# Macaron block on one core: turned exponentials by VectorE instead of TensorE and ScalarE, keys and values by separate products, the latent stored interleaved

## The chip, the core and the metric

The kernel runs on one core of one Trainium2 chip. The metric is the device time of one execution in microseconds (us); lower is better. In the rows, PE is TensorE (PEld its weight loads), DVE is VectorE, ACT is ScalarE, POOL is GpSimd and SP is SyncE, whose queue issues the loads and stores.

## What is computed

Input x has 8 batches of 512 tokens of 256 features. The block is a feed-forward part at half weight, an attention part, and the same feed-forward part again with the same weights:

```
x = x + 0.5 * ffn(layernorm(x))
x = x + attn(layernorm(x))        # softmax over the 8 groups of a query and a key token
x = x + 0.5 * ffn(layernorm(x))

ffn(x):   # H = 16 heads, HD = 16, L = 64, E = 8 experts
    h   = rmsnorm(x) * gamma1
    q   = (h @ Wq + bq).reshape(b, t, 16, 16)
    kv  = ((h @ Wdown + bdown) @ Wup + bup).reshape(b, t, 16, 32)
    k, v = split(kv)
    att = softmax(einsum('bthd,btgd->bthg', q, k) / sqrt(16))     # within ONE token: head h against head g
    out = einsum('bthg,btgd->bthd', att, v).reshape(b, t, 256)
    x   = x + out @ Wo + bo
    h2  = rmsnorm(x) * gamma2
    return x + sum over e of softmax(h2 @ Wg + bg)[e] * (h2 @ We[e])
```

All of it is in float32. The large products of the feed-forward part are made of a rounded high part and a rest (`_hi`, `_lo`), so that each takes three matmuls of TensorE's rounded float32 type.

The part that is changed is the small attention inside `ffn`: each token has its own 16 x 16 scores. The latent is `h @ Wdown + bdown`, 64 numbers for each token.

## The kernel before

**Jobs and pairs.** A feed-forward pass over one batch (512 tokens, NT = 4 tiles of 128) is a job. Jobs 0 to 7 are the first feed-forward part, 8 to 15 the second; the attention over all batches lies between. A job's per-token attention works in two pairs of tiles (`p` = 0, 1), so there are 32 pairs, `c = 2 * job + p`.

**Order.** Every piece of work is a step with an engine, a cost in ns and the steps that it waits for (`all_steps`). `all_orders` plays them through and gives each engine a fixed order: whenever an engine is free, it takes the ready step of the highest rank. The tables `SOONER` (an addition to the rank by name) and `FIRST` (by job) shift the ranks. PSUM banks 5, 6 and 7 go round among the steps in `RING`; banks 3 and 4 together go to those in `WIDE`; banks 0 to 2 go round among the experts. On the chip, each engine works through its list strictly in that order and waits at semaphores.

**One pair, before.** Its steps are, with the lines of the profile:

1. `down` (PE), `la_hi` (ACT L1258), `la_lo` (DVE L1041, L1043) and `la_one` (POOL L1572) make the latent `la` for the whole job, 64 rows high part and 64 rows rest, column = token.
2. `kv` (PE, `psum<-wu,la` and `psum<-wu,la_one`): for each tile two matmuls of 512 columns, keys and values of one tile together, into banks 3 and 4.
3. `kv_turn` (DVE L1064, L1066): two stream transposes, one for keys and one for values, into one of three buffers `kvc`. A stream transpose turns each 32 x 32 block in place.
4. `expand` (ACT L1260 and POOL L1512, four operations each by the string `EXPAND`): the turned keys and values times a mask, into `kvx`.
5. `scores` (PE L662): 32 small products. `top` (DVE L1076, L1080): subtracts the maximum. `exp` (ACT L1264).
6. `turn_probs` (PE L789): four 128 x 128 transposes of the exponentials into a bank of the ring. `at` (ACT L1275): four copies from there into `at`, the weights of the next product.
7. `attend` (PE L673): 32 small products into banks 3 and 4, with the sum of the exponentials as a 17th column. `mult` (DVE L1089, L1091): reciprocal of the sum, and the product with it into `on`. `out_turn` (DVE L1100): a stream transpose into `ot`.
8. `oT` (PE L803), `wo` (PE `psum<-wo,oT`), `x1`, `half` (DVE L1116) and so on, up to the experts: 16 steps `expert` for each job (PE L491 `psum<-we,h`, six matmuls of 512 columns each), which DVE (`add`, L1165) and ACT (`y`, L1339) empty in turn.

`turn_nothing` (PE L702) is a number of transposes whose result nobody reads.

## Time and profile before

| | before |
|---|---|
| median of 3 runs | 1039.59 us (1038.6 to 1041.17) |
| the profiled execution's own time | 1039.06 us |
| its span (first to last instruction) | 1037.2 us |
| PE busy | 986.5 us, 95% |
| DVE busy | 823.4 us, 79% |
| POOL busy | 768.3 us, 74% |
| ACT busy | 675.7 us, 65% |

Busy time is the union of an engine's instructions; consecutive matmuls overlap, so the duration of one (272 ns for a 128-column transpose) is longer than the distance from its start to the next one's start. What a group of matmuls takes of TensorE is read as the distance between starts in the timeline. The profile is of one execution, so what follows is reckoned against its 1039.06 us, 1.86 us more than its span.

### The profile page before, as it was taken

The numbers are of one execution on the slowest core, as the hardware profiler recorded it, in microseconds if no ns is written. First come the engines' busy times: TensorE is split into PE (matmuls) and PEld (weight loads), VectorE is DVE, ScalarE is ACT, GpSimd is POOL, SyncE is SP. The second block draws the span as 40 slices with busy tenths as digits, with TensorE's granted clock in tenths as the row PEclk, the third lists the DMA queues.
The fourth block names the chain that finished last, engine by engine and source line by source line (L and its number), as shares of the span: only waits on it lengthen the run. The fifth ranks groups of instructions, "written<-read, shape, count | busy, mean of one in ns | idle before, by whom it ended". The sixth has DMA issues, their size and how long they took to land.

```text
span 1037.2 us, 28141 instructions
## 1 busy us (share of the span) xinstructions
PE 986.5 (95%) x11200; PEld 769.0 (74%) x11200; DVE 823.4 (79%) x1239; ACT 675.7 (65%) x1411; POOL 768.3 (74%) x789
## 2 busy tenths in 40 slices
PE   7699999999999989999999999888999999999998
PEld 6578778888788766667667667556788788888786
DVE  7588788788877459999999999997877877776754
ACT  4586575675776357778778777686775665755752
POOL 7777787786774549899899898997676775865734
PEclk8799999999999999999999999999999999999999
DMA  6210000000000000000000000000000000000001
GB/s 195 84 43 1 2 2 1 3 2 1 2 2 2 1 1 2 2 2 1 2 1 3 2 2 2 2 1 2 3 1 23 22 2 22 22 2 22 22 2 41
DMA packets 7966, 14.20 MB, mean 14 GB/s; under 512 B 1945, under 2 KB 5660, under 8 KB 7838
## 3 DMA queue, kind: packets, MB, share of 16 engines
q1 hardware_dynamic: 7838, 12.41, 3.6%
q8 instruction: 91, 1.49, 0.6%
q14 instruction: 37, 0.30, 0.1%
HBM read 8.21 MB, written 4.19 MB: 12 GB/s over the span
## 4 chain that ended last, share of the span: by engine, by line
PE 70%; DVE 10%; POOL 5%; issue 5%; ACT 3%; DVEq 0%; ACTq 0%; POOLq 0%
PE psum L491 48%; PE psum L892 5%; PE psum L902 4%; PE psum L918 4%; DVE oT L1191 3%; DVE late L1197 3%; PE psum L662 2%; PE psum L673 2%; POOL kvx L1585 1%; PE psum L803 1%; PE psum L818 1%; POOL late L1585 1%; PE psum L789 1%; DVE hT L1183 1%; POOL rs L1478 1%
## 5 line engine op out<-in xcount | busy, mean ns | idle before, releaser
L491 PE MATMUL psum<-we,h 128*128 128x512 f32 x1536 | 393.6, 400 | 1.8 <-DVE X L1165 1.2
L491 PEld LDWEIGHTS psum<-we,h 128*128 128x128 f32 x1536 | 278.1, 188 | 63.7 <-issue 2.9
L1401 ACT ACTIVATE kvx<-psum 128x1024 f32<-128x1024 f32 x126 | 129.1, 1025 | 62.2 <-PE psum L902 60.5
L1339 ACT ACTIVATE late<-psum,gate 128x256 f32<-128x256 f32 x252 | 104.9, 468 | 97.4 <-PE psum L491 51.6
L1165 DVE SCALAR_TENSOR_TENSOR X<-psum,gate,X 128x256 f32<-128x256 f32 x260 | 124.4, 479 | 54.0 <-PE psum L491 42.3
L1191 DVE TENSOR_REDUCE oT<-psum 128x128 fp32r<-128x1024 f32 x128 | 154.7, 1219 | 14.7 <-PE psum L892 14.4
L1543 POOL TENSOR_TENSOR late<-late 128x512 f32<-128x512 f32 x63 | 81.4, 1293 | 111.1 <-ACT late L1339 111.1
L1197 DVE TENSOR_REDUCE late<-kvx 128x256 f32<-128x2048 f32 x63 | 143.4, 2276 | 0.3 <-POOL late L1585 0.2
L1585 POOL TENSOR_TENSOR kvx<-kvx,late 128x2048 f32<-128x2048 f32 x32 | 125.3, 3916 | 16.4 <-ACT late L1408 16.3
L1585 POOL TENSOR_TENSOR late<-kvx,late 128x2048 f32<-128x2048 f32 x31 | 121.8, 3928 | 19.7 <-ACT late L1408 19.7
L1260 ACT ACTIVATE kvx<-kvcs,mask 128x512 f32<-128x512 f32 x132 | 86.4, 730 | 37.7 <-DVE kvcs L1066 35.2
L902 PE MATMUL psum<-oT,neg_id 128*128 128x512 f32 x256 | 88.6, 427 | 13.6 <-DVE oT L1191 13.3
L1512 POOL TENSOR_SCALAR kvx<-kvcs,mask 128x512 f32<-128x512 f32 x124 | 85.9, 713 | 8.4 <-DVE kvcs L1066 8.3
L902 PEld LDWEIGHTS psum<-oT,neg_id 128*128 128x128 f32 x256 | 40.6, 188 | 28.5 <-DVE oT L1191 19.2
L1275 ACT ACTIVATE at<-psum 64x256 f32<-64x256 f32 x128 | 48.5, 379 | 17.3 <-PE psum L789 15.8
L892 PEld LDWEIGHTS psum<-late 32*128 32x128 f32 x1024 | 36.7, 185 | 27.0 <-issue 27.0
L892 PEld LDWEIGHTS psum<-kvcs 32*128 32x128 f32 x1024 | 36.7, 185 | 26.5 <-issue 23.9
L491 PEld LDWEIGHTS psum<-wq,hT 128*128 128x128 f32 x384 | 51.8, 198 | 5.4 <-issue 2.6
L491 PE MATMUL psum<-wq,hT 128*128 128x256 f32 x384 | 53.5, 290 | 2.1 <-DVE hT L1035 2.0
L1290 ACT ACTIVATE late<-late 128x256 f32<-128x256 f32 x64 | 26.2, 411 | 44.2 <-DVE late L1111 44.2
L1548 POOL TENSOR_TENSOR X<-X,late 128x256 f32<-128x256 f32 x63 | 46.6, 740 | 9.0
L892 PE MATMUL psum<-kvcs 32*128 32x128 f32 x1024 | 49.3, 295 | 3.1 <-ACT kvx L1401 2.4
(169 smaller groups left out, 1950.9 us busy)
## 6 DMA issues: line engine op xcount, KB each, us to landing
X<-in_L_attn_hidden_states SPq DMA_DIRECT2D x8, 512.0 KB, 5.5
out<-X SPq DMA_DIRECT2D x7, 512.0 KB, 2.6
X<-in_L_ffn_We SPq DMA_DIRECT2D x2, 1024.0 KB, 10.7
out<-X SPq DMA_DIRECT2D x1, 384.0 KB, 2.3
kvx<-in_L_ffn_Wq SPq DMA_DIRECT2D x1, 256.0 KB, 3.4
kvx<-in_L_ffn_Wup SPq DMA_DIRECT2D x2, 128.0 KB, 3.0
kvx<-in_L_ffn_Wo SPq DMA_DIRECT2D x8, 32.0 KB, 2.6
X<-in_L_attn_Wk SPq DMA_DIRECT2D x1, 256.0 KB, 2.6
```

Source lines behind the costliest of these rows:

```text
L491: ins = e.matmul(out_ap, l, r, start=(n == 0), stop=(n == len(terms) - 1))
L892: ins = e.matmul(psum[:, pair(half) + bank, n * HQN:(n + 1) * HQN], qk[b % 2][rows, 1, hg, m * P:(m + 1) * P], qk[b % 2][rows, 0, hg, q0:q ...
L902: ins = e.matmul(psum[:, bank, :].rearrange("p (g n) -> p g n", n=HQN), neg_id[:, :], mr[g // 2 % 2][:, queries(g)].unsqueeze(1).to_broadc ...
L1165: e.scalar_tensor_tensor(out=xi, in0=psum[:, u % 3, w * D:(w + 1) * D], scalar=gate[k % 2][:, i, 2 * n + w:2 * n + w + 1], in1=xi, op0=ALU ...
L1191: e.tensor_reduce(mr[g // 2 % 2][:, queries(g)], heads(g), AX.X, ALU.max).then_inc(a_max, 1)
L1197: e.tensor_reduce(rec[u % 2][:, :], exponentials(u)[:, :, :], AX.X, ALU.add).then_inc(a_total, 1)
L1260: expand(e, k, "A", lambda o, src, m_: e.activation(o, src, ACT.Copy, scale=m_))
L1339: e.activation(y[:, n // 2 * 2 + w, :], psum[:, u % 3, w * D:(w + 1) * D], ACT.Copy, scale=gate[k % 2][:, i, 2 * n + w:2 * n + w + 1]).the ...
L1401: e.activation(exponentials(u)[:, queries(g), :], heads(g), ACT.Exp, scale=float(D) ** -0.5).then_inc(a_exp, 1)
L1512: expand(e, k, "P", lambda o, src, m_: e.tensor_scalar(o, src, m_, 1.0, ALU.mult, ALU.mult))
L1543: own.step(e.tensor_tensor(y[:, 0:2, :], y[:, 0:2, :], y[:, 2:4, :], ALU.add))
L1585: e.tensor_tensor(prob[u % 2][:, :, :].rearrange("p g n -> p n g"), exponentials(u)[:, :, :], rec[u % 2][:, :].unsqueeze(2).to_broadcast([ ...
```

## The change

- `turn_probs` is gone. `at` is now on DVE: two stream transposes, each of 64 partitions x 512, from the exponentials in SBUF straight into `at`. For this the order of tokens in the small products, the permutation `perm` and the rows of `Wo` (reordered before the launch, so that one load replaces eight) are other ones.
- `kv` becomes `key` for each pair (four matmuls of 256 columns, a bank of the ring) and `val` for each job (eight matmuls of 256 columns, banks 3 and 4). `kv_turn` becomes `key_turn` for each pair (one transpose) and `val_turn` for each job (two). `expand` becomes `key_P`, `key_A`, `val_P`, `val_A` (two operations each, of the same 128 x 512). The keys' half of `kvx` is free again after the `scores` two pairs before, no longer after the `attend`.
- The latent is written interleaved: the four tiles' columns lie side by side (`by_tile`), so that `la_hi` and `la_lo` write, and `key` reads its weights, at every fourth word. `val` reads its weights in one piece.
- `mult` and `out_turn` change places: `out_turn` turns the raw 544 columns out of PSUM into `raw_ot` (SBUF), which frees banks 3 and 4, and `mult` then takes reciprocal and product from SBUF to SBUF.
- One of the four groups of `turn_nothing` at the start (13 transposes ahead of the second `attend`) is gone. `SOONER` and `FIRST` are new tables.

```diff
-EXPAND = "PPAAAPPA"
+EXPAND = {"key": "PPAA", "val": "APPA"}
...
-            put("PE", 945, ("kv", s, p), ("la_lo", s, part(p)), ("la_one", s, part(p)), ...)
-            put("DVE", 2005, ("kv_turn", s, p), ("kv", s, p), ...)
+            put("PE", 470, ("key", s, p), ("la_lo", s, part(p)), ("la_one", s, part(p)), ...)
+            put("DVE", 1030, ("key_turn", s, p), ("key", s, p))
...
-            put("PE", 435, ("turn_probs", c), ("exp", c), ("attend", c - 1))
-            put("ACT", 1450, ("at", c), ("turn_probs", c))
-            put("PE", 1085, ("attend", c), ("at", c), ("mult", c - 1))
-            put("DVE", 1000, ("mult", c), ("attend", c), ("out_turn", c - 1))
-            put("DVE", 700, ("out_turn", c), ("mult", c), ("oT", s - 1, p))
+            put("DVE", 1450, ("at", c), ("exp", c), ("attend", c - 1))
+            if not p:
+                put("PE", 940, ("val", s), ("la_lo", s, part(1)), ("la_one", s, part(1)), ...)
+                put("DVE", 2005, ("val_turn", s), ("val", s), ...)
+            put("PE", 1085, ("attend", c), ("at", c), *((f"val_{w}", c) for w in "PA"), ("out_turn", c - 1))
+            put("DVE", 750, ("out_turn", c), ("attend", c))
+            put("DVE", 900, ("mult", c), ("out_turn", c), ("oT", s - 1, p))
...
-                elif piece == ("attend", 1):
-                    turn_nothing(e, 13)
...
+                elif name == "val":
+                    e.wait_ge(s_la_one, done(k))
+                    e.wait_ge(s_la_lo, done(k))
+                    for i in range(NT):
+                        cols = slice(i * P, (i + 1) * P)
+                        terms = [(la[:, cols], wu[:, 0, D:]), (la_one[:, cols], wu[0:HALF + 2, 1, D:])]
+                        ins = product(e, psum[:, 3 + i // 2, (i % 2) * D:(i % 2 + 1) * D], terms)
+                    ins.then_inc(s_val, 1)
...
+        def by_tile(t):
+            return t[:, :].rearrange("p (n i) -> p i n", i=NT)
...
-                    own.step(e.tensor_tensor(la[up, cols], psum[low, b, cols], la[low, cols].bitcast(F32), ALU.subtract))
-                    e.wait_ge(own.sem, own.n)
-                    e.tensor_tensor(la[up, cols], psum[up, b, cols], la[up, cols].bitcast(F32), ALU.add).then_inc(s_la_lo, 1)
+                    own.step(e.tensor_tensor(kept[up], made[low], kept[low].bitcast(F32), ALU.subtract))
+                    e.wait_ge(own.sem, own.n)
+                    e.tensor_tensor(kept[up], made[up], kept[up].bitcast(F32), ALU.add).then_inc(s_la_lo, 1)
...
+                elif name == "at":
+                    c = piece[1]
+                    if c:
+                        e.wait_ge(s_attend, c)
+                    else:
+                        e.wait_ge(s_pad, 4)
+                    e.wait_ge(s_exp, c + 1)
+                    for z in range(2):
+                        half = slice(z * HALF, (z + 1) * HALF)
+                        ins = e.transpose(at[half, :, z, :].rearrange("p (u n) h -> p n u h", u=2),
+                                          ex[c % 2][half, :].rearrange("p (n g) -> p n g", g=NR))
+                    ins.then_inc(s_at, 1)
...
+                    src = psum[:, 3:5, 0:NR // 2 * (HD + 1)].rearrange("p a (t d) -> p d a t", d=HD + 1)
+                    e.transpose(raw_ot, src).then_inc(s_raw, 1)
+                elif name == "mult":
...
+                    own.step(e.reciprocal(r_, raw_ot[:, HD]))
+                    e.wait_ge(own.sem, own.n)
+                    e.tensor_tensor(ot[c % 2][:, :, :].rearrange("p z (d h) -> p d z h", h=H), raw_ot[:, 0:HD],
+                                    r_.unsqueeze(1).to_broadcast([P, HD, 2, H]), ALU.mult).then_inc(s_ot, 1)
```

**TensorE's order in the middle of the first feed-forward part, before.** The names are those of the tiles: `kvx,qc` is `scores`, `kvx,at` is `attend`, `ident,late` is `turn_probs` where four stand alone, `we,h` the experts, `ident,ct` a transpose of the gate, `ident,xs` of the next job's input.

```order
L662 MATMUL psum<-kvx0,qc0 32x64 x32
L831 MATMUL psum<-ident,ct 128x16 x4
L491 MATMUL psum<-we,h21 128x512 x6
L491 MATMUL psum<-we,h20 128x512 x6
L789 MATMUL psum<-ident,late 128x128 x4
L491 MATMUL psum<-we,h20 128x512 x6
L662 MATMUL psum<-kvx1,qc1 32x64 x32
L673 MATMUL psum<-kvx0,at 32x68 x32
L491 MATMUL psum<-we,h20 128x512 x6
L789 MATMUL psum<-ident,late 128x128 x4
L749 MATMUL psum<-ident,xs 128x128 x8
```

The same place of a job in the changed kernel:

```order
L677 MATMUL psum<-kvx0,qc0 32x64 x32
L505 MATMUL psum<-we,h20 128x512 x24
L677 MATMUL psum<-kvx1,qc1 32x64 x32
L687 MATMUL psum<-kvx0,at 32x68 x32
L505 MATMUL psum<-we,h20 128x512 x12
L761 MATMUL psum<-ident,xs 128x128 x4
L818 MATMUL psum<-perm,late 128x8x16 x4
L761 MATMUL psum<-ident,xs 128x128 x4
L505 MATMUL psum<-we,h20 128x512 x6
L687 MATMUL psum<-kvx1,at 32x68 x32
```

The two rows of four transposes per job are gone; from the first `scores` to the first `attend` stand four expert steps instead of three, and there are again three places in a job where small products begin behind large ones.

**VectorE's order at the same place, before.** `mx` is `top`, `rc` and the row behind it `mult`, `late<-late` `out_turn`, `X<-psum,gate` `add`, which empties an expert's bank.

```order
L1076 TENSOR_REDUCE mx1<-psum 128x32
L1080 TENSOR_TENSOR late<-psum,mx1 128x512
L1089 RECIPROCAL rc<-psum 128x32
L1091 TENSOR_TENSOR late<-psum,rc 128x512
L1100 STREAM_TRANSPOSE late<-late 128x16x2x16
L1165 SCALAR_TENSOR_TENSOR X<-psum,gate1,X 128x256 x2
```

And in the changed kernel, where `at<-late` is the new `at` and `late<-psum 128x544` the new `out_turn`:

```order
L1126 STREAM_TRANSPOSE at<-late 64x16x2x16 x2
L1210 SCALAR_TENSOR_TENSOR X<-psum,gate0,X 128x256 x4
L1111 TENSOR_REDUCE mx1<-psum 128x32
L1115 TENSOR_TENSOR late<-psum,mx1 128x512
L1135 STREAM_TRANSPOSE late<-psum 128x544
L1142 RECIPROCAL rc<-late 128x32
L1144 TENSOR_TENSOR late<-late,rc 128x16x2x16
L1126 STREAM_TRANSPOSE at<-late 64x16x2x16 x2
L1210 SCALAR_TENSOR_TENSOR X<-psum,gate0,X 128x256 x2
```

Each pair has one more row of VectorE (two instructions of `at`) ahead of the `add` that empties an expert's bank, and the rows of `mult` stand behind the transpose instead of ahead of it.

## Rows read from the trace of the kernel before

**Rows 1.** The page: busy time of each engine, and the chain that ended last.

```profile
PE 986.5 (95%) x11200; PEld 769.0 (74%) x11200; DVE 823.4 (79%) x1239; ACT 675.7 (65%) x1411; POOL 768.3 (74%) x789
...
PE 70%; DVE 10%; POOL 5%; issue 5%; ACT 3%; DVEq 0%; ACTq 0%; POOLq 0%
```

**Rows 2.** The chain in order of time: start, length (us), what; one piece of each job.

```profile
201.16 13.55 PE psum L491 x76
...
241.70 13.55 PE psum L491 x76
...
828.26 13.55 PE psum L491 x76
...
869.03 13.56 PE psum L491 x76
```

**Rows 3.** Busy us of PE, PEld, DVE, ACT, POOL in those two stretches; PEclk.

```profile
201.16:241.70 40.54, 40.51 (x453) 33.41 (x453) 32.86 (x67) 25.67 (x62) 30.29 (x44) 1.00 0.01 2
828.26:869.03 40.77, 40.54 (x454) 33.42 (x453) 31.18 (x59) 25.67 (x63) 28.70 (x40) 1.00 0.04 15
```

**Rows 4.** Timeline of PE around the two turn_probs of a job: start, length.

```profile
228.20 0.60 PE L789 MATMUL psum<-ident,late 128*128 128x128 f32 x4
228.55 1.63 PE L491 MATMUL psum<-we,h 128*128 128x512 f32 x6
...
233.64 0.63 PE L789 MATMUL psum<-ident,late 128*128 128x128 f32 x4
234.11 1.04 PE L749 MATMUL psum<-ident,xs 128*128 128x128 f32 x8
```

**Rows 5.** Timeline of PE: matmuls of 512 and of 256 columns.

```profile
205.20 1.56 PE L491 MATMUL psum<-we,h 128*128 128x512 f32 x6
206.60 1.56 PE L491 MATMUL psum<-wo,oT 128*128 128x256 f32 x12
207.99 1.09 PE L491 MATMUL psum<-hT,wd 128*128 128x512 f32 x4
```

**Rows 6.** Timeline of PE: first matmul of a kv, and what follows its four.

```profile
220.57 0.40 PE L491 MATMUL psum<-wu,la 128*128 128x512 f32 x1
...
221.52 0.85 PE L491 MATMUL psum<-h,wg 128*16 128x512 f32 x3
```

**Rows 7.** DVE, 201.16 to 241.70, by line: busy us, mean ns, idle before.

```profile
L1064 DVE STREAM_TRANSPOSE kvcs<-psum 128x512 f32<-128x512 f32 x2 | 2.3, 1136 | 0.0
...
L1100 DVE STREAM_TRANSPOSE late<-late 128x512 f32<-128x512 f32 x2 | 2.2, 1086 | 0.2
...
L1091 DVE TENSOR_TENSOR late<-psum,rc 128x512 f32<-128x512 f32 x2 | 1.4, 692 | 0.1
...
L1041 DVE TENSOR_TENSOR la<-psum,la 64x512 fp32r<-64x512 f32 x1 | 0.7, 685 | 0.0
```

**Rows 8.** Timeline: half (DVE) and rms2 (POOL) in two jobs.

```profile
92.27 1.19 DVE L1116 SCALAR_TENSOR_TENSOR X<-late,X 128x1024 f32<-128x1024 f32 x1
...
92.87 0.65 POOL L1536 TENSOR_SCALAR rms<-ssq 128x4 f32<-128x4 f32 x1 [0.64 <-ACT late L1290]
...
208.99 1.23 DVE L1116 SCALAR_TENSOR_TENSOR X<-late,X 128x1024 f32<-128x1024 f32 x1
...
210.12 0.20 POOL L1536 TENSOR_SCALAR rms<-ssq 128x4 f32<-128x4 f32 x1 [2.13 <-ACT late L1290]
```

**Rows 9.** Timeline of job 0 (ACT, PE) and job 8 (ACT); in brackets idle before.

```profile
29.86 0.61 ACT L1264 ACTIVATE late<-late 128x512 f32<-128x512 f32 x1
31.80 1.55 ACT L1275 ACTIVATE at<-psum 64x256 f32<-64x256 f32 x4 [1.33 <-PE psum L789]
...
51.48 1.58 PE L702 MATMUL psum<-ident 128*128 128x128 f32 x13
53.00 1.15 PE L673 MATMUL psum<-kvx,at 128*32 128x68 f32 x64
...
704.54 0.77 ACT L1275 ACTIVATE at<-psum 64x256 f32<-64x256 f32 x2 [0.87 <-PE psum L789]
```

**Rows 10.** The page: the maximum over groups in the attention (1024 PSUM words by partition).

```profile
L1191 DVE TENSOR_REDUCE oT<-psum 128x128 fp32r<-128x1024 f32 x128 | 154.7, 1219 | 14.7 <-PE psum L892 14.4
```

283 lines of the change are left out of this document (147 added, 136 removed).

## Prediction

> **What bounds the kernel now.** I read the page first: TensorE is busy 95% of the span, VectorE 79%, GpSimd 74%, and the chain that ended last runs 70% through TensorE [rows 1]. Then the chain in order of time. In both feed-forward parts it repeats the same long piece of expert matmuls once for each job: at 201.16 and 241.70, so 40.54 us a job, and at 828.26 and 869.03, so 40.77 us [rows 2]. Then the busy time in just those two stretches: TensorE 40.51 of 40.54 and 40.54 of 40.77 at a granted clock of 1.00, VectorE 32.86 and 31.18, ScalarE 25.67 in both, GpSimd 30.29 and 28.70 [rows 3]. The reader is to see that in a settled job nothing but TensorE's own work sets the time. What is taken from TensorE there shortens the kernel one for one, as long as no other engine comes up to its 40 us. VectorE is the nearest, 7.7 us below. In jobs 0 and 8 it is different: there the experts of an earlier job are missing as filling, and TensorE waits for the steps of the pair.
>
> **What the change takes from TensorE.** A job has two `turn_probs`. By the distance between starts the first takes 228.55 - 228.20 = 0.35 us and the second 234.11 - 233.64 = 0.47 us, since the next group's weights come later there [rows 4]. Together 0.82 us. I count 14 settled jobs (1 to 7 and 9 to 15): 14 x 0.82 = 11.5 us. Job length then would be 39.7 and 39.95 us.
>
> The split products cost nothing by rows. Six matmuls of 512 columns take 206.60 - 205.20 = 1.40 us, twelve of 256 columns 207.99 - 206.60 = 1.39 us, with new weights for each [rows 5]: the price is by column. A `kv` takes 221.52 - 220.57 = 0.95 us [rows 6], 1.90 for a job; four plus four plus eight matmuls of 256 columns take 16 x 0.116 = 1.86. No row shows a weight load that reads every fourth word. At worst each of the 8 in a job costs one more product's time, 0.93 us a job, which would eat the whole gain; at best nothing. I take nothing, because the loads run ahead under the product before them, as in rows 5.
>
> Small products begin behind large ones at three places in a job both before and after, so changing between them costs the same.
>
> **What it puts on VectorE**, for a job. Two transposes of `at` for each pair, four in a job. No row has a transpose that both reads and writes in order. The upper bound is the transpose from SBUF to SBUF, 1.09 us, the lower the plain operation of 512 words, 0.69 [rows 7]: 2.8 to 4.4 us. `out_turn` now handles 544 words out of PSUM: between 0.73 (0.692 x 544 / 512) and 1.21 (1.136 x 544 / 512) against 1.09 [rows 7], so -0.7 to +0.2 for two. For a plain read, hopping through PSUM costs nothing: 1024 words take 1.219 us in the maximum over groups [rows 10], 1.23 in `half`, which reads SBUF in order [rows 8]. Key and value turns are four transposes as before: nothing. `mult` keeps its two instructions: nothing by itself. `la_lo` writes at every fourth word: 0.685 each [rows 7] at best; at worst the ratio 1.09 / 0.69 more, +0.8 for two. The sum is +2.1 to +5.4 us. VectorE then has 35.0 to 38.3 us of work in a job of 39.7. I take 1.09 for `at`, the nearest row (it too writes in runs of 16 words), and the middle for the rest: +4.5, so 37.4. That is 94%: below TensorE, but with little room.
>
> [...]
>
> **A new collision.** The product in `mult` used to read PSUM and a small SBUF tensor; now both inputs lie in SBUF. The one operation of that kind in a job is `half`. When GpSimd had a 0.20 us operation start under it, that operation took 0.65 us and ended at 93.52, just behind `half` at 93.46; in a later job it started at the end of `half` and took 0.20 [rows 8]. So they exclude each other. In the feed-forward part GpSimd is busy 75% of the time with 44 instructions of 0.69 us on average [rows 3]; a `mult` waits for half of one with that chance, 0.26 us, and GpSimd waits as long for it. That is 0.5 us a job for VectorE, 37.9 in all. The Trainium skill (SBUF — State Buffer, section SBUF: two separate sides) names this as a lock that VectorE and GpSimd hold for a whole instruction; rows 8 agree.
>
> Queued behind `at` and `mult` on VectorE are the `add`s that empty an expert's bank. While VectorE waits (`at` for the exponentials on ScalarE, `mult` for GpSimd), TensorE runs on two more expert steps, 2.8 us, and then stops. Half of VectorE's spare time is used up, so some of this will reach TensorE. I take about one such collision a job, 0.3 us, 14 x 0.3 = +4.2 us; the bounds are 0 and the 0.82 of rival 2.
>
> **What is gone from ScalarE** (two times 1.55 us a job [rows 9]) is hidden, as it has 15 us to spare [rows 3]. Expansion is in eight equal operations as before, split four and four: nothing.
>
> **Jobs 0 and 8.** There the way over TensorE is waited for: ScalarE stood idle 1.33 us before `at` in job 0 and 0.87 in job 8 [rows 9]. Both go: -2.2 us. The transposes in place of the 1.55 us of copies [rows 9] take 1.4 to 2.2 us: nothing. The 13 filling transposes took 53.00 - 51.48 = 1.52 us [rows 9]; part of that may have filled a wait that stays, so I count -1.0. Keys get to `scores` one transpose earlier, but the values now wait for the whole latent; I set these off against each other, with 2 us either way.
>
> **Sum:** 1039.06 - 11.5 - 2.2 - 1.0 + 4.2 = 1028.6 us. The profiled execution is 0.5 us below the median of 1039.59, which changes nothing here.
>
> **The rivals.**
> 1. *All of it comes through and more.* VectorE's additions vanish in its spare time (-4.2), the starts gain 2 us more, and ScalarE's relief frees expert banks sooner: about 1021. For it speaks that TensorE waits for nobody in the settled jobs now.
> 2. *The gain is given back.* TensorE's 0.82 a job turns into waiting: for the latent, whose two VectorE writes may be 0.8 us longer in a chain that ends at `key`, or for slower weight loads, or for expert banks behind `at`. The job stays at 40.5 us, only the starts gain: 1039.06 - 3.2 = 1036.
> 3. *VectorE becomes the bound, the kernel gets slower.* Today it is idle 7.7 us in a job. If half of that, 3.9, is waiting which its order cannot avoid (for a product that has just been made, for ScalarE's half of a step), a job takes 37.4 + 3.9 = 41.3 us instead of 40.54: 14 x 0.8 = +11, less the 3.2 of the starts: 1047. It decides from the point at which VectorE's work and those waits together exceed 40.5 us; at 1.09 us for each new transpose that is 3.2 us of waits. Against it: a VectorE that waits for a full TensorE loses nothing by having more to do meanwhile.
> 4. *The transposes leave TensorE but their time was hidden anyway.* Excluded by rows 3: TensorE has 0.03 us idle in the job.
>
> **How the numbers follow.** Forecast (1023 to 1033) 0.45, rival 1 0.15, rival 2 0.22, rival 3 0.18. A measurement of this kernel tells a change from none at about 0.3%, 3.1 us. Faster: 0.45 + 0.15 + half of rival 2 = 0.71. The same: the other half, 0.11. Slower: 0.18. The range goes from 1018, rival 1 with the starts' 2 us and a little more, to 1045, most of the way to rival 3: some 0.05 lies below and 0.13 above.
>
> **What the profile afterwards would show.** Right: the expert piece of the chain repeats every 39.7 to 40.1 us in the middle of both parts, TensorE idle under 0.4 us there, VectorE at 36 to 38.5 us. `at` at 0.7 to 1.1 us each; `out_turn` under 1.2. `mult`'s product sometimes well over 0.69, or GpSimd operations stretched under it. The first `at` of job 0 done before 33.35 us, where it ended so far. Rival 2: job length 40.5, with TensorE waiting before `psum<-wu,la` for `la_lo`, or its 256-column matmuls with `la` further apart than 0.12. Rival 3: TensorE idle before the experts because of VectorE's `add`, VectorE above 39 us. What would make me wrong altogether is a new order that starves TensorE in places which the settled jobs of before say nothing of, above all jobs 0 and 8.

## The result, and the profile after

The changed kernel takes 1044.96 us (median of four runs, 1044.74 to 1045.93) against 1039.3 us before on the same chip: a ratio of 1.0053, 95% interval 1.0041 to 1.0066. A later comparison gave 1.0057 (1.0041 to 1.0074). It is slower, by 5.5 to 6 us, where 11 us less were forecast. The profiled execution took 1045.93 us, with a span of 1044.1. One execution of all those below, 3174.89 us in run e3, fell in a slow state and is left out of its ratio, though not of its median of five.

The page: busy time of each engine, and the chain that ended last.

```profile
PE 994.7 (95%) x11187; PEld 781.9 (75%) x11187; DVE 876.1 (84%) x1303; ACT 642.4 (62%) x1283; POOL 772.8 (74%) x789
...
PE 71%; DVE 17%; issue 6%; POOL 3%; ACT 2%; DVEq 0%; ACTq 0%; POOLq 0%
```

Against [rows 1] TensorE has 13 instructions less in sum and is busy 8.2 us longer. Something that it still does has become dearer, and by more than the 11.5 us that `turn_probs` took. VectorE is busy 53 us more, and its part of the chain went from 10% to 17%.

The chain in order of time (start, length, what), with one piece of each job:

```profile
162.68 10.79 PE psum L505 x58
...
245.69 10.79 PE psum L505 x58
...
879.06 10.00 PE psum L505 x60
920.32 10.00 PE psum L505 x60
```

Between the first two lie two jobs, so a job takes 83.01 / 2 = 41.5 us, and 41.26 in the second feed-forward part; before it was 40.54 and 40.77 [rows 2]. The busy time in these two stretches (PE, PEld, DVE, ACT, POOL, then PEclk):

```profile
162.68:245.69 83.01, 82.36 (x905) 67.87 (x905) 71.00 (x141) 47.17 (x109) 61.50 (x88) 1.00 0.01 2
879.06:920.32 41.26, 41.01 (x453) 33.95 (x454) 34.52 (x63) 23.82 (x55) 28.65 (x40) 1.00 0.04 15
```

TensorE is still full (82.36 of 83.01) and VectorE has 35.5 us a job, not 37.4. So the settled job is not bound by VectorE, as rival 3 had it, and the reader has to look inside TensorE's own work. Its timeline at one pair's `key` (four products) and the `val` behind it (eight):

```profile
181.03 0.51 PE L505 MATMUL psum<-wu,la 128*128 128x256 f32 x1
181.38 0.40 PE L505 MATMUL psum<-wu,la_one 66*128 66x256 f32 x1
181.61 0.40 PE L505 MATMUL psum<-wu,la 128*128 128x256 f32 x1
...
182.07 0.28 PE L505 MATMUL psum<-wu,la 128*128 128x256 f32 x1
...
182.31 0.29 PE L505 MATMUL psum<-wu,la 128*128 128x256 f32 x1
```

From the third product of `key` to the first of `val`, 182.07 - 181.61 = 0.46 us for two products, 0.23 each. Within `val`, 182.31 - 182.07 = 0.24 for two, 0.12 each, the pitch of [rows 5]. The same products, the same columns, the granted clock at 1.00 in both; they differ in the weights, which `key` takes at every fourth word of the latent and `val` from adjacent ones. The first product takes 0.12 us more (181.38 - 181.03 = 0.35). A job has two `key`, so it pays 8 x 0.115 = 0.92 us, which is the very bound of the prediction that I set aside.

VectorE in 162.68 to 245.69 (two jobs), by line and form; busy us, mean ns:

```profile
L1126 DVE STREAM_TRANSPOSE at<-late 64x512 f32<-64x512 f32 x8 | 5.6, 695 | 0.1
...
L1144 DVE TENSOR_TENSOR late<-late,rc 128x512 f32<-128x512 f32 x4 | 3.2, 789 | 0.1
L1135 DVE STREAM_TRANSPOSE late<-psum 128x544 f32<-128x544 f32 x4 | 3.0, 742 | 0.0
...
L1067 DVE TENSOR_TENSOR la<-psum,la 64x512 fp32r<-64x512 f32 x2 | 2.2, 1088 | 2.0 <-ACT la L1303 2.0
L1069 DVE TENSOR_TENSOR la<-psum,la 64x512 fp32r<-64x512 f32 x2 | 2.2, 1083 | 0.1
```

The new transposes are at the lower end of my bounds (0.70 us), and `la_lo` is at the upper (1.09 instead of 0.69). ScalarE's `la_hi`, which I had not priced, went from 0.58 to 1.10 us too (from 120 to 340 us):

```profile
L1303 ACT ACTIVATE la<-psum 64x512 fp32r<-64x512 f32 x5 | 5.5, 1095 | 1.1 <-PE psum L505 1.1
```

Two places outside the settled jobs stand out. In job 0 (start, length; DVE, then POOL, then PE):

```profile
32.43 5.42 DVE L1144 TENSOR_TENSOR late<-late,rc 128x512 f32<-128x512 f32 x1
...
30.56 2.76 POOL L1547 TENSOR_SCALAR kvx<-kvcs,mask 128x512 f32<-128x512 f32 x4
33.28 0.43 POOL L981 TENSOR_SCALAR kvx<-mask 128x128 f32<-128x128 f32 x1
33.58 3.71 POOL L1528 TENSOR_TENSOR we<-X,we 128x512 fp32r<-128x512 f32 x3
...
37.99 0.63 PE L818 MATMUL psum<-perm,late 128*128 128x128 f32 x4 [3.50 <-DVE late L1144]
```

The product in `mult` lasts 5.42 us, where the others take a median of 0.70. It begins during the third of eight GpSimd instructions that stand one against the other (four `kvx`, one mask, three `we`), and ends at 37.85, just behind the last of them, which ends at 37.29. TensorE waits 3.50 us for it.

And at the passage from the attention to job 8, where TensorE comes to `attend` 16 late:

```profile
709.85 2.04 PE L687 MATMUL psum<-kvx,at 128*32 128x68 f32 x64 [2.79 <-issue]
...
728.06 0.48 PE L505 MATMUL psum<-wu,la 128*128 128x256 f32 x1 [1.71 <-DVE la L1069]
```

The busy time of the stretch behind it (PE, PEld, DVE, ACT, POOL, then PEclk):

```profile
710.00:715.00 5.00, 5.00 (x135) 4.83 (x131) 2.74 (x5) 1.51 (x4) 4.41 (x9) 0.50 0.01 3
```

Before `attend` 16 TensorE is idle for 2.79 us; from 710 to 715 the granted clock then stands at 0.50, its lower level of 1.2 GHz. Before the change the stretches from 700 to 720 us all show 1.00. On VectorE, job 9's statistics and a turn of keys now stand ahead of `top` 16. At 728.06 TensorE waits 1.71 us for `la_lo`.

### The profile page after: what moved, and what is told of

The parts are those of the page before. It is cut to its first block, busy times and chain, and to the rows that moved or that the text cites. A ratio compares the mean times of both kernels' runs of the same rounds, so it can differ in the third digit from the quotient of the medians.

```text
span 1044.1 us, 28145 instructions
## 1 busy us (share of the span) xinstructions
PE 994.7 (95%) x11187; PEld 781.9 (75%) x11187; DVE 876.1 (84%) x1303; ACT 642.4 (62%) x1283; POOL 772.8 (74%) x789
## 4 chain that ended last, share of the span: by engine, by line
PE 71%; DVE 17%; issue 6%; POOL 3%; ACT 2%; DVEq 0%; ACTq 0%; POOLq 0%
PE psum L505 49%; PE psum L907 5%; PE psum L917 4%; PE psum L933 4%; DVE oT L1236 3%; DVE late L1242 3%; PE psum L687 2%; PE psum L677 2%; DVE at L1126 2%; DVE X L1210 2%; PE psum L818 1%; PE psum L833 1%; POOL late L1624 1%; DVE kvcs L1100 1%; DVE late L1135 1%
## 5 line engine op out<-in xcount | busy, mean ns | idle before, releaser
L1624 POOL TENSOR_TENSOR kvx<-kvx,late 128x2048 f32<-128x2048 f32 x32 | 125.5, 3923 | 16.5 <-ACT late L1443 16.4
L917 PEld LDWEIGHTS psum<-oT,neg_id 128*128 128x128 f32 x256 | 40.5, 188 | 29.6 <-DVE oT L1236 20.3
L505 PE MATMUL psum<-wo,oT 128*128 128x256 f32 x384 | 51.6, 284 | 1.9 <-DVE oT L1150 1.9
L505 PEld LDWEIGHTS psum<-wo,oT 128*128 128x128 f32 x384 | 48.7, 189 | 4.9 <-issue 2.5
```

What stands on the lines that cost most here:

```text
L505: ins = e.matmul(out_ap, l, r, start=(n == 0), stop=(n == len(terms) - 1))
L917: ins = e.matmul(psum[:, bank, :].rearrange("p (g n) -> p g n", n=HQN), neg_id[:, :], mr[g // 2 % 2][:, queries(g)].unsqueeze(1).to_broadc ...
L1624: e.tensor_tensor(prob[u % 2][:, :, :].rearrange("p g n -> p n g"), exponentials(u)[:, :, :], rec[u % 2][:, :].unsqueeze(2).to_broadcast([ ...
```

## The experiments

The expectations name theories by letters. W: TensorE's weight loads set the time. V: VectorE does. C: the granted clock costs it at jobs 0 and 8. O: the order of VectorE's steps at job 8 does. X: the product of pair 0 waits for GpSimd.

Each ratio is to runs of the kernel before on the same chip. Where two versions are set against each other, it is by these ratios, and the changed kernel stands at 1.0055, the middle of its two comparisons.

| run | what | us | ratio, 95% |
|---|---|---|---|
| e12 | changed kernel once more | 1044.17 | 1.0057 (1.0041 to 1.0074) |
| e1 | key reads adjacent words | 1034.68 | 0.9959 (0.9944 to 0.9974) |
| e2 | latent stored plainly | 1029.13 | 0.9911 (0.9897 to 0.9926) |
| e3 | product first, out of PSUM | 1043.59 | 1.0043 (1.0028 to 1.0059) |
| e4 | filling ahead of attend 1 and 16 | 1042.35 | 1.0044 (1.0027 to 1.0060) |
| e5 | four transposes back at each pair | 1053.87 | 1.0159 (1.0137 to 1.0180) |
| e6 | kernel before, kv at every fourth word | 1040.40 | 1.0023 (1.0013 to 1.0032) |
| e7 | top 16 ahead of the statistics | 1044.60 | 1.0064 (1.0049 to 1.0079) |
| e8 | two latents | 1033.06 | 0.9953 (0.9938 to 0.9967) |
| e9 | e8 with filling at three places | 1029.03 | 0.9910 (0.9893 to 0.9926) |
| e10 | e9 with the rules of e7 and e3 | 1035.84 | 0.9966 (0.9953 to 0.9979) |
| e15 | latent written in stored order | 1037.87 | 0.9997 (0.9987 to 1.0006) |
| e16 | e9 with the rule of e7 | 1032.99 | 0.9952 (0.9935 to 0.9969) |
| e17 | e9 written in stored order | 1030.80 | 0.9914 (0.9898 to 0.9931) |
| e18 | e15 with the filling | 1036.53 | 0.9977 (0.9967 to 0.9986) |
| e20 | product first in pair 0 alone | 1039.47 | 1.0014 (1.0001 to 1.0027) |
| e19 | e9 with that | 1027.90 | 0.9894 (0.9874 to 0.9914) |

**The changed kernel again: e12.**

> The changed kernel itself once more, beside the two below and on the same chip, so that they can be set against it without going over the kernel before. 1042 to 1046 us, ratio 1.004 to 1.007.

It came out as before. In its profile the first expert of job 8 begins at 730.10 us, in the first one at 732.45, so two profiles of one kernel differ by 2 us at this place.

**The weight loads: e1.**

```diff
-                        terms = [(by_tile(la)[:, i], wu[:, 0, 0:D]), (by_tile(la_one)[:, i], wu[0:HALF + 2, 1, 0:D])]
+                        whole = parts_of(k, B) == 1
+                        own_cols = slice(i * P, (i + 1) * P)
+                        first, one = (la[:, own_cols], la_one[:, own_cols]) if whole else (by_tile(la)[:, i], by_tile(la_one)[:, i])
+                        terms = [(first, wu[:, 0, 0:D]), (one, wu[0:HALF + 2, 1, 0:D])]
```

> The changed kernel, except that in the 14 whole jobs (1 to 7 and 9 to 15) the key product takes its weights from the latent in one adjacent piece of 128 words instead of every fourth word. The latent is still stored interleaved, so the keys of these jobs belong to the wrong tokens; all else is as it was. Theory W (the weight load at every fourth word is what takes the gain back): key's eight 256-column matmuls of a job go from 0.235 to 0.12 us, 0.92 us a job, and the wait of 0.1 to 0.3 us ahead of the first goes too: 14 x 1.0 to 1.2 = 14 to 17 us, so 1028 to 1031 us and a job of 40.4 us. Rival V (VectorE with its new transposes, longer latent writes and the exclusion with GpSimd sets the job's length, the slow loads lie in time that would be waited anyway): 1042 to 1046 us, with TensorE idle more before the experts and attend.

From 1.0055 to 0.9959: 10 us faster, where I expected 14 to 17. Timeline of PE at the same `key`:

```profile
179.01 0.39 PE L505 MATMUL psum<-wu,la 128*128 128x256 f32 x1
179.24 0.28 PE L505 MATMUL psum<-wu,la_one 66*128 66x256 f32 x1
179.36 0.28 PE L505 MATMUL psum<-wu,la 128*128 128x256 f32 x1
```

The pitch is 0.12 us again. Two jobs of the first part and one of the second:

```profile
161.16:242.33 81.17, 80.65 (x906) 66.15 (x905) 70.55 (x141) 46.72 (x109) 61.81 (x88) 1.00 0.01 2
866.83:907.21 40.38, 40.20 (x453) 33.12 (x454) 34.21 (x63) 23.68 (x55) 28.86 (x40) 1.00 0.04 15
```

A job takes 40.58 and 40.38 us, 0.92 and 0.88 less than in the changed kernel. Fourteen times that is more than 10 us; the profiled execution took 1030.90 us, 3.8 less than the median. The loads are the largest loss. But with them repaired a job of the first part is still as long as before the change (40.54), though its two `turn_probs` are gone: here TensorE is idle for 0.26 us a job instead of 0.03, and busy only 0.2 us less. This is a second loss, of which more below.

**The latent's layout as a whole: e2.**

```diff
         def by_tile(t):
-            return t[:, :].rearrange("p (n i) -> p i n", i=NT)
+            return t[:, :].rearrange("p (i n) -> p i n", i=NT)
```

> The changed kernel with the latent stored in the plain order: la_hi, la_one and la_lo write, and key and val read, one adjacent piece for each tile, in all 16 jobs. Queries, keys and values then pair the wrong tokens; the amount of work is the same. Theory W: the gain is that of the plain key load (1028 to 1031 us), with up to 2 us more at jobs 0 and 8, whose latent is on the way that is waited for: 1026 to 1031. Rival V: VectorE is relieved by 2 x 0.4 us a job of la_lo, and GpSimd and ScalarE by 0.3 and 0.5 us, so if VectorE's load sets the job's length this gives at least 14 x 0.4 = 5 us more than the key load alone, 1023 to 1026 if both matter, about 1038 if only VectorE does.

15 us faster than the changed kernel, and 5 faster than e1. The key loads alone are not all that the interleaving costs.

**The load by itself: e11.** Behind TensorE's last instruction:

```diff
+            for hop in (1, 2, 4):
+                for wide in (128, 256, 512):
+                    for n in range(24):
+                        o = n % hop
+                        w_ = la[:, :].rearrange('p (n i) -> p i n', i=hop)[:, o, n % (4 // hop) * P:n % (4 // hop) * P + P]
+                        e.matmul(psum[:, 3, 0:wide], w_, wu[:, 0, 0:wide], start=True, stop=True, skip_group_check=True)
```

> The changed kernel with nine runs of 24 products each put behind TensorE's last instruction, with the latent as weights and nothing to wait for, written to a bank that nobody reads: weights taken in adjacent words, at every second and at every fourth word, each with products of 128, 256 and 512 columns. Only their pitch counts, not the kernel's time. Theory W: adjacent, the pitch is by columns, 0.06, 0.12 and 0.23 us; at every fourth word the load lasts 0.235 us whatever follows, so 0.235 for 128 and for 256 columns, and 0.235 to 0.25 for 512, where it is covered; every second word in between or like adjacent. Rival (a fixed time added to each load): at every fourth word 0.12 us above the adjacent pitch at each width, 0.18, 0.235 and 0.35.

One row for each run of 24 products, from its first start to that of the next (busy PE and PEld, with those that overlap an edge counted on both sides; then PEclk): adjacent, every second and every fourth word, each with 128, 256 and 512 columns.

```profile
1039.74:1042.36 2.62, 2.62 (x24) 2.62 (x24) 1.00 0.31 115
1042.36:1045.27 2.91, 2.91 (x27) 2.91 (x26) 1.00 0.00 0
1045.27:1050.88 5.61, 5.61 (x26) 4.54 (x25) 1.00 0.00 0
1050.88:1053.70 2.82, 2.82 (x26) 2.81 (x24) 1.00 0.03 6
1053.70:1056.66 2.96, 2.96 (x27) 2.96 (x27) 1.00 0.00 0
1056.66:1062.26 5.60, 5.60 (x27) 4.75 (x25) 1.00 0.00 0
1062.26:1067.69 5.43, 5.43 (x25) 5.43 (x25) 0.87 0.00 0
1067.69:1073.35 5.66, 5.66 (x25) 5.66 (x26) 0.53 0.00 0
1073.35:1078.88 5.53, 5.53 (x24) 5.53 (x24) 1.00 0.00 0
```

The last row ends with the start of its 24th product, so that 23 pitches lie in it; the others are divided by 24: adjacent words 0.109, 0.121 and 0.234 us; every second word 0.118, 0.123 and 0.233; every fourth word 0.226, 0.236 and 5.53 / 23 = 0.240. So every second word costs next to nothing, and at every fourth a load lasts 0.23 us whatever its product's columns. It is a duration of the load, hidden under a product that is as long, and not a fixed addition; the rival's 0.18 and 0.35 are not there. With 128 columns even adjacent words give 0.109, where I expected 0.06 by columns: the pitch does not follow the columns down to there. In the two rows ahead of the last the granted clock falls to its lower level while nothing but such loads and short products ran, and the pitch stays at 0.23: the load does not go with that clock.

**The same load under a longer product: e6**, an edit of the kernel before.

```diff
-                        terms = [(la[:, i * P:(i + 1) * P], wu[:, 0, :]),
-                                 (la_one[:, i * P:(i + 1) * P], wu[0:HALF + 2, 1, :])]
+                        mixed = lambda t: t[:, :].rearrange("p (n i) -> p i n", i=NT)[:, i]
+                        plain = lambda t: t[:, i * P:(i + 1) * P]
+                        of_tile = mixed if parts_of(k, B) == 1 else plain
+                        terms = [(of_tile(la), wu[:, 0, :]), (of_tile(la_one), wu[0:HALF + 2, 1, :])]
```

> The kernel before the change, whose kv product (512 columns for each weight load) reads its weights at every fourth word of the latent in the 14 whole jobs. The latent is stored as before, so those keys and values belong to the wrong tokens; the amount of work is the same. Theory W, as I now see it (a load at every fourth word takes 0.235 us, which the product of 512 columns before it, 0.235 us, just covers, and one of 256 columns, 0.117 us, does not): 1038 to 1041 us, no change, with loads of about 0.31 us and kv at 0.95 to 1.05 us. Rival (each such load adds a fixed time of its own, whatever runs before it): 16 loads a job x 0.115 us would be 1.8 us a job, 14 jobs, +26 us; half of it, if it adds 0.06, +13.

Its loads by form between 201 and 282 us (busy us, mean ns):

```profile
L491 PEld LDWEIGHTS psum<-wu,la_one 66*128 66x128 f32 x8 | 2.5, 313 | 0.0
L491 PEld LDWEIGHTS psum<-wu,la 128*128 128x128 f32 x8 | 2.5, 309 | 0.1
```

These are eight slow loads a job, as many as the changed kernel has for its keys (the 16 of the expectation was a slip, so the rival would have been +13 us). They cost 2.4 us in all, 0.02 for each of 14 x 8: nearly hidden, where under 256 columns each costs 0.115. Two things together make the loss: the interleaving and the split of `kv` into products of 256 columns.

**The writes: e15.** The same latent, written word after word, with the hop moved to the reading of PSUM:

```diff
-                    made = psum[:, b, :].rearrange("p (i n) -> p i n", i=NT)[:, tiles]
-                    kept = by_tile(la)[:, tiles]
+                    made = psum[:, b, :].rearrange("p (i n) -> p n i", i=NT)[:, :, tiles]
+                    kept = la[:, :].rearrange("p (n i) -> p n i", i=NT)[:, :, tiles]
...
-                    e.activation(by_tile(la)[0:L, span(tiles)], psum[0:L, b, :].rearrange("p (i n) -> p i n", i=NT)[:, span(tiles)],
-                                 ACT.Copy).then_inc(s_la_hi, 1)
+                    e.activation(la[:, :].rearrange("p (n i) -> p n i", i=NT)[0:L, :, span(tiles)],
+                                 psum[0:L, b, :].rearrange("p (i n) -> p n i", i=NT)[:, :, span(tiles)], ACT.Copy).then_inc(s_la_hi, 1)
```

> The changed kernel, but la_hi and la_lo go through the same interleaved latent in the order in which it is stored, so that they write adjacent words and hop in what they read from PSUM; the key loads still read every fourth word. Nothing that is computed changes. Theory W: la_lo goes from 1.07 back to 0.69 to 0.75 us and la_hi from 1.10 towards 0.58, so VectorE has 0.7 us a job less, and the time hardly follows, since TensorE's key loads set the job: 1041 to 1045 us, the gain of 0 to 3 us at jobs 0 and 8, where the latent is waited for. Rival V: 14 x 0.3 to 0.7, 4 to 10 us faster than the changed kernel, 1035 to 1040. If reading by hops from PSUM is as dear as writing by hops to SBUF, la_lo stays at 1.0 to 1.1 and the time at 1044.

By form, from 120 to 340 us, and the busy time of two jobs of the first part and one of the second:

```profile
L1069 DVE TENSOR_TENSOR la<-psum,la 64x512 fp32r<-64x512 f32 x5 | 3.5, 695 | 0.2
L1067 DVE TENSOR_TENSOR la<-psum,la 64x512 fp32r<-64x512 f32 x5 | 3.4, 684 | 2.6 <-ACT la L1303 2.6
...
L1303 ACT ACTIVATE la<-psum 64x512 fp32r<-64x512 f32 x5 | 2.9, 586 | 1.1 <-PE psum L505 1.1
```

```profile
162.27:244.53 82.26, 81.76 (x905) 67.97 (x905) 69.55 (x141) 46.35 (x109) 61.49 (x88) 1.00 0.01 2
871.75:912.91 41.16, 40.96 (x453) 33.97 (x454) 33.45 (x63) 23.30 (x55) 28.60 (x40) 1.00 0.04 15
```

All three are at their old price, and 6 us are gained, as rival V said and not theory W, although TensorE was full in the settled jobs. The job shortens from 41.5 to 41.1 in the first part and from 41.26 to 41.16 in the second, some 3 us in all; the rest lies at the starts. The likely way is the chain `down`, `la_hi`, `la_lo`, `key`, which is 0.5 + 2 x 0.4 = 1.3 us shorter; no run separates it from the relief of VectorE. This edit alone brings the changed kernel level with the kernel before.

**Is TensorE still the bound: e5.**

```diff
                 elif name == "attend":
+                    turn_nothing(e, 4, 3)
```

> The changed kernel with four TensorE transposes of the identity ahead of each of the 32 attends, in the place and number of the turn_probs that the change took away, read by nobody and waiting for nobody. Theory W (TensorE still bounds the settled job): all of their time is added, 32 x 0.35 to 0.47 = 11 to 15 us, so 1056 to 1060 us. Rival V (VectorE bounds it): TensorE has time to spare in a job and they are hidden in part, 1045 to 1050 us.

By the ratios 10.8 us are added (the intervals allow 7 to 14), 0.34 for each of 32, where the expectation had 11 to 15. In the profile a job grows by 0.75 us in the first part (84.51 us for two) and by 0.51 in the second (41.77), not by 0.82. So most of the time of four transposes is paid where they stand, and the 11.5 us that I took for `turn_probs` are the right size, a little high.

**Two latents: e8** (only the core of the edit; the steps `la_turn` on ScalarE and `one_turn` on GpSimd go to the planner too, at 1100 and 700 ns, and some small constants move to make room).

```diff
-                        terms = [(by_tile(la)[:, i], wu[:, 0, 0:D]), (by_tile(la_one)[:, i], wu[0:HALF + 2, 1, 0:D])]
+                        terms = [(stored(la, k)[:, i], wu[:, 0, 0:D]), (stored(la_one, k)[:, i], wu[0:HALF + 2, 1, 0:D])]
...
+                    one, other = la, la_one
+                    if parts_of(k, B) == 1:
+                        e.wait_ge(s_la_turn, turned(k))
+                        e.wait_ge(s_one_turn, turned(k))
+                        one, other = la_in_turn, one_in_turn
...
+                elif name == "la_turn":
+                    e.wait_ge(s_la_lo, done(k))
+                    e.activation(by_tile(la_in_turn), stored(la, k), ACT.Copy).then_inc(s_la_turn, 1)
...
+                elif name == "one_turn":
+                    e.tensor_scalar(by_tile(one_in_turn), stored(la_one, k).bitcast(F32), 1.0, 1.0, ALU.mult, ALU.mult).then_inc(s_one_turn, 1)
```

> The changed kernel, nothing that is computed changed, but in the 14 whole jobs the latent is stored in the plain order, and one ScalarE copy and one GpSimd copy make a second, interleaved one for the values; so no weight load of key or val hops. Jobs 0 and 8 are as they were. It puts about 1.1 us on ScalarE and 0.7 us on GpSimd in each job and takes 0.8 us of the latent's writes from VectorE. Theory W: it keeps what the plain key load gave (10 us, although its keys belonged to the wrong tokens) or a little more, as the plain latent did: 1029 to 1036 us, a job of 40.4 to 40.8 us. Rival (the second copy comes late for val, or GpSimd, already at 75 to 80% in a job, now holds up the exponentials' or the experts' sums): 1037 to 1044 us.

It keeps the gain of e1 with nothing computed differently: 0.9953, 10.5 us below the changed kernel.

**Clock and filling: e4, e9.**

```diff
+                elif piece == ("attend", 1):
+                    turn_nothing(e, 13)
+                elif piece == ("attend", 2 * B):
+                    turn_nothing(e, 30)
+                elif piece == ("oT", 0, 0):
+                    turn_nothing(e, 20)
```

e4 has the first two in the changed kernel, e9 all three in the one with two latents.

> The changed kernel with TensorE transposes of the identity that nobody reads put back: 13 ahead of attend 1 (job 0) and 30 ahead of attend 16 (job 8), where TensorE is idle for 2.8 us and its granted clock then stands at 0.50 for some 7 us. Nothing that is computed changes. Theory C (the clock that falls after idle time costs the starts several us): the stretch after attend 16 stays at 1.00 and job 8 gets 2 to 4 us back, and 0 to 1.5 us in job 0: 1039 to 1043 us. Rival O (the order of VectorE's steps at job 8 sets the delay, the clock is hidden in it): 1044 to 1046.

> The kernel with two latents (a plain one for the keys, an interleaved copy for the values) with TensorE transposes that nobody reads put ahead of three pieces that wait in jobs 0 and 8: 13 ahead of attend 1, 20 ahead of the first transpose of the attention output in job 0, 30 ahead of attend 16. Nothing that is computed changes. Theory C (clock): the stretch from 705 to 710 us no longer shows 0.66, nor 30 to 45 us 0.72 to 0.75; 2 to 4 us less than the 1033.1 us of the two latents: 1029 to 1031. Rival (the slow clock lies in time that is waited for anyway): 1032 to 1034.

In the changed kernel 1 us (intervals that overlap), with two latents 4.5 us (intervals apart). The stretch from 710 to 715 us in e4, which had 0.50 in the changed kernel; then the slow stretch of e8, and the same in e9:

```profile
710.00:715.00 5.00, 3.88 (x143) 3.35 (x142) 3.39 (x6) 2.29 (x5) 4.41 (x9) 1.00 0.02 5
...
705.00:710.00 5.00, 4.35 (x92) 3.94 (x81) 3.08 (x5) 1.53 (x4) 4.49 (x9) 0.66 0.02 3
...
705.00:710.00 5.00, 3.33 (x114) 2.76 (x104) 3.60 (x6) 1.88 (x4) 4.57 (x8) 1.00 0.01 3
```

The clock is back in both. The time hardly follows. From e8 to e9 the first expert of job 0 comes 0.5 us earlier (53.35, 52.86) and that of job 8 0.6 (723.72, 723.12), while the spans differ by 2.9 us. The rest lies in settled jobs, where no filling stands: e8 has two waits of TensorE in the middle of an `attend` that wait for nothing the profile shows, 2.6 us together, and e9 has none there:

```profile
818.24 0.43 PE L712 MATMUL psum<-kvx,at 128*32 128x68 f32 x11 [1.07 <-issue]
...
940.33 0.55 PE L712 MATMUL psum<-kvx,at 128*32 128x68 f32 x20 [1.52 <-issue]
```

The two profiles of the changed kernel have them too, each time at the same two places (0.75 and 0.60 us, 0.56 and 1.07). So theory C holds for the clock and for some 0.6 us of time; most of what separates these two profiles came another way. Whether the fillings remove these waits, and how, no run shows.

**The order at job 8: e7, e16, e10.** The edit of e7 is one more thing that the statistics of job 9 wait for, `("top", 2 * B)`; e16 puts it into e9, e10 puts it and the edit of e3 there.

> The changed kernel with one more rule for the planner: VectorE's statistics of job 9 come after the maximum over groups (top) of pair 16. Nothing that is computed changes. Theory O (the order of VectorE at job 8, statistics and key's turns ahead of top, delays attend 16 by 2.8 us and with it the clock): the first expert of job 8 comes 2 to 4 us earlier than the 732.45 us of the changed kernel, 1041 to 1043 us in all. Rival (what waits at job 8 is the whole latent, then val, its turns and its expansion, and top was not on that path): 1044 to 1046 us.

> The two latents with the three fillings, and VectorE's statistics of job 9 after top 16. Nothing that is computed changes. It tells apart which of two parts made the version with both 7 us slower than the one with neither: if it is this rule of order, 1034 to 1037 us, with the first expert of job 8 at 728 to 731 us; if it is the product with the reciprocal ahead of the transpose, 1028 to 1030 us.

> The one above with two more parts: VectorE's statistics of job 9 after top 16, and the product with the reciprocal ahead of the transpose to tokens, out of PSUM, as before the change. Nothing that is computed changes. If each keeps what it seemed to give alone (0 to 1.5 us each): 1027 to 1030 us. Rival (the two only moved the order about, and the planner's new order loses as much elsewhere): 1030 to 1033.

e7 changes nothing: its first expert of job 8 begins at 729.12 us, hardly sooner than in e12. e16 is 4 us slower than e9, with that expert at 729.32 instead of 723.12, and e10 differs from e16 by 1.4 us, within the intervals. So it is this rule that costs, and theory O falls: that VectorE's order is late for `attend` 16 can be read, but pulling one step forward repairs nothing.

**The product out of PSUM: e3, e20, e19.** In e3 for all pairs, in e20 and e19 for pair 0 alone:

```diff
+                    if c == 0:
...
+                        e.tensor_tensor(on.rearrange("p (a t d) -> p a t d", a=2, d=HD), ps[:, :, :, 0:HD],
+                                        r_.unsqueeze(3).to_broadcast([P, 2, NR // 2, HD]), ALU.mult).then_inc(s_raw, 1)
```

> The changed kernel with one part undone: the product with the reciprocal comes first and reads PSUM, as before the change, and the transpose to tokens follows it out of SBUF. Nothing that is computed changes. Theory W (TensorE's weight loads take the gain, VectorE is beside the path): between 1043 and 1047 us, the same as the changed kernel within 2 us. Rival V (the exclusion of the SBUF product with GpSimd, measured at 0.28 us for each of 32, reaches TensorE): 3 to 9 us faster, 1036 to 1042, with less waiting of TensorE ahead of the transposes of the attention output.

> The changed kernel, in which pair 0 alone takes the product with the reciprocal first, out of PSUM, and then the transpose, as before the change; the other 31 pairs and the planned order are untouched. Nothing that is computed changes. In the profile of the changed kernel the product of pair 0, with both inputs in SBUF, lasts from 32.43 to 37.85 us instead of 0.69, while GpSimd runs one instruction behind the other. Theory X (VectorE gets no turn until GpSimd pauses): the product takes 0.69 us again, TensorE's first transpose of the attention output comes some 3.5 us sooner, and 2 to 4 us are left at the end: 1040 to 1042. Rival (GpSimd then has to be waited for instead, and nothing is left): 1044 to 1045.

> The two latents with the three fillings, and pair 0 with the product first, out of PSUM. Nothing that is computed changes. The product of pair 0 takes 5.66 us there. Theory X: 2 to 4 us less than the 1029.0 us of that kernel: 1025 to 1027. Rival: 1028.5 to 1030.

e3 gains 1 us, within the uncertainty: what the product saves (0.28 us on average) the transpose out of SBUF takes back (1.07 instead of 0.75 us). At the start its gain is there, the first long piece of experts in the chain begins at 115.19 us instead of 119.92, and later jobs lose half of it. e20 changes one of 32 and gains 4 us by the ratios; there that piece begins at 115.87, and the lead of 4 us lasts to the end. DVE in job 0 of e20, and the transposes on PE that waited 3.50 us before:

```profile
31.49 0.69 DVE L1140 TENSOR_TENSOR late<-psum,rc 128x512 f32<-128x512 f32 x1
32.22 1.08 DVE L1152 STREAM_TRANSPOSE late<-late 128x512 f32<-128x512 f32 x1
...
34.23 0.66 PE L819 MATMUL psum<-perm,late 128*128 128x128 f32 x4
```

TensorE starts them at 34.23 instead of 37.99, and its wait is gone. With both inputs in SBUF the product did not end until GpSimd's row of instructions had; read out of PSUM it takes 0.69 us beside the same row. e19 is 1.6 us below e9, with intervals that overlap, where 2 to 4 were expected; its profiled span is 1023.3 against 1027.0. It is the fastest version measured, 1.06% below the kernel before.

**Do the causes add: e17, e18.** Both write in stored order and have the filling; e17 has two latents, e18 one.

> The two latents with the three fillings, and every interleaved latent (la_hi, la_lo of jobs 0 and 8, and both copies in the other jobs) written in the order in which it is stored, so that the writes are adjacent and the reads hop. Nothing that is computed changes. If the write is what is dear, as the last run showed for reads out of PSUM (0.69 in place of 1.09 us on VectorE, 0.59 in place of 1.10 on ScalarE), the ScalarE copy goes from 1.14 to about 0.6 us, and 1 to 2 us are gained at jobs 0 and 8: 1026 to 1029 us. If reading SBUF by hops is as dear as writing, the copies stay at 1.1 us and the time at 1028 to 1030.

> The changed kernel with the latent written in stored order and the three fillings, with no second latent: the key loads hop. Nothing that is computed changes. If the three causes add (loads 8 to 10 us, writes 6, clock and order at jobs 0 and 8 2 to 4): 1034 to 1036 us, so that it lies 6 to 9 us above the version with two latents of this call. If the fillings gain nothing once the latent is early: 1037 to 1038.

Both came 0.5 to 0.8 us above what was expected if all goes well. They differ by 6.5 us, so the key loads cost about that even when the latent comes early. Against e9, e17 gains nothing: the plain latent of its whole jobs was never written by hops, and its copy, which now reads SBUF by hops, takes as long as one that writes by hops (1134 ns in e9):

```profile
L1354 ACT ACTIVATE la_in_turn<-la 128x512 fp32r<-128x512 f32 x14 | 16.2, 1159 | 2.1 <-DVE la L1106 1.9
```

The causes do not add: 10 (loads) + 6 (writes) + 4 (the product) + 1 to 4.5 (filling) is more than the 16.5 us by which the forecast missed.

## Why the prediction was wrong

**The step that failed** is "The split products cost nothing by rows ... I take nothing, because the loads run ahead under the product before them". Rows 5 have loads of adjacent words. I had the upper bound, "0.93 us a job, which would eat the whole gain", and the trace of after has 0.92: a load at every fourth word takes 0.23 us and is not hidden under 256 columns. The choice between the bounds rested on a row in which the thing that was in doubt, the hop, did not occur; between ends far apart it should at least have carried the weight of a forecast of its own. This makes rival 2 the one that came nearest in mechanism ("slower weight loads", "latent late"), but its price was too low: the job did not stay at 40.5, it went to 41.5.

**A second term that was too small** is "about one such collision a job, 0.3 us". The loads alone would bring a job to 39.72 + 0.92 = 40.64 and 39.95 + 0.92 = 40.87 us; it is 41.5 and 41.26. With the loads repaired in e1, what is left above the forecast without collisions is 40.58 - 39.72 = 0.86 us in the first part and 40.38 - 39.95 = 0.43 in the second, 9 us in all against the 4.2 that I took. Which waits these are, the runs do not separate.

**The latent's writes.** For `la_lo` I had 0 to +0.8 us of VectorE's time, took the middle, and said that VectorE had room. The size is the upper bound, 0.8. What I missed is the place: this is latency in the chain to `key`, together with `la_hi`, which I did not price at all (+0.5). Written in stored order it costs nothing, and 6 us come back (e15).

The Trainium skill (Vector Engine (DVE) Microarchitecture Reference, section 5.2 Measured stream behaviour) has 1.054 ns a word where a port's words come in runs of at least two, and 1.71 to 2.51 ns where a write hops at every word. By these figures each `la_lo` would take an estimated 0.3 to 0.7 us more, and the trace has 0.40; `at`, which writes in runs, would take an estimated 0.6 us, and the trace has 0.70. On both terms the page is nearer than what I took from the nearest rows, 0.2 and 1.09.

**A new collision.** I took 0.26 us for each `mult` as a mean over chances. The mean is 0.28 (972 - 691 ns), but that it agrees is luck. One instruction in job 0 takes 5.42 us, half of the whole sum, and 4 us of the kernel's end with it; the other 31 wait 0.14 us on average, and their median takes 0.70. "A `mult` waits for half of one" fails in job 0: there it waited through the last six of eight GpSimd instructions in a row.

The Trainium skill (SBUF — State Buffer, section SBUF: two separate sides) speaks of a lock held "for the whole instruction"; the trace, with a wait of 4.7 us across six instructions, goes beyond that.

**VectorE** has 35.5 us a job instead of 37.4: four `at` at 0.70 are 2.8 and not 4.4, two `out_turn` at 0.74 give 0.7 back. Rival 3 was argued with a sum that was 2 us too high.

**What the change takes from TensorE** was nearly right as a price: 10.8 us for 32 in e5, 11.5 for 28 in the forecast. But it did not come out of the job. In e1 TensorE is busy 0.2 us a job less than before in the first part and 0.34 in the second, instead of 0.82, and a job is as long as before in the first (40.58 against 40.54) and 0.39 shorter in the second (40.38 against 40.77); the forecast was 0.52 in both.

**Jobs 0 and 8.** -3.2 us were forecast. In job 0 the hop over TensorE did go, the first `at` ends at 27.5 instead of 33.35 us, and the first expert began 2 us later all the same, because of the product above. At job 8 the first expert begins at 732.45 us instead of 724.62. That the new order might starve TensorE there is what I named as making me "wrong altogether"; the idle 2.79 us, the clock behind it and the late latent are shown. e8, with its latents repaired and no filling, has that expert at 723.72 already, although it still waits 2.80 us and has the slow clock.

**The forecast's number came out in e9 by luck.** With these losses mended, e9 comes to 1029.0 us and e19 to 1027.9, where the forecast was 1028.6. But the forecast had 7.3 us of its gain in 14 settled jobs (11.5 - 4.2) and 3.2 at the starts. In e9 three jobs of the first part take 122.91 us:

```profile
160.04:282.95 122.91, 118.99 (x1359) 99.37 (x1358) 104.50 (x212) 73.10 (x168) 94.81 (x136) 1.00 0.01 2
...
231.33 3.00 PE L507 MATMUL psum<-we,h 128*128 128x512 f32 x12 [2.33 <-DVE X L1247]
```

That is 40.97 a job, 0.43 longer than before, with TensorE idle for 1.3 us of it; the longest wait is for VectorE's `add`, the sign that the prediction had given for rival 3. (e1, which has no second latent, has 40.58 there and waits for the `add` for only 0.17.) In the second part a job takes 40.31 us, 0.46 shorter than before. Over seven jobs of each part the two cancel. The 10 us by which e9 beats the kernel before lie in and around the first jobs of each part: by its first gate product (`psum<-h,wg`) e9 is 5.4 us ahead at job 3, 2.2 at job 7, 2.0 at job 8, 8.0 at job 10 and 9.8 at job 15. The passage over the attention, from job 7 to job 8, is 0.3 us longer than before by the same mark (4.9 in the changed kernel).

What stays open: which step of the order makes VectorE late for the `add` in the first part, and why the starts gain more than was forecast. A layout in which neither keys nor values need more than every second word was not tried.

## What to carry to other kernels

When a product is split so that each weight load has fewer columns above it, the load's own duration can come out: price it, and with it the layout that it reads, before counting the split as free. Where a layout has to be changed, put the hop where it is free: here that was the reading of PSUM by VectorE and ScalarE, not the write to SBUF and not the weight load. An operation of VectorE with both inputs in SBUF should not stand where the path waits for it while GpSimd works without a pause. And where a repaired kernel meets the forecast, compare its jobs with the forecast's terms before taking the sum as confirmed.
